# A new opening for a Perceiver layer kernel: the order of the first loads, of the first block's splitting and of the query rows

## What is computed

```python
qh = (q @ Wq.T + bq).reshape(B, Sq, N_HEAD, D_HEAD)      # q = layernorm(x), 128 x 256
kh = (k @ Wk.T + bk).reshape(B, Sk, N_HEAD, D_HEAD)      # k = v = context, 12544 x 256
vh = (v @ Wv.T + bv).reshape(B, Sk, N_HEAD, D_HEAD)
scores = jnp.einsum('bqhd,bkhd->bhqk', qh, kh) / np.sqrt(D_HEAD)
scores = jnp.where(attention_mask[:, None, :, :], NEG_FILL, scores)
probs = jax.nn.softmax(scores, axis=-1)
out = jnp.einsum('bhqk,bkhd->bqhd', probs, vh)
```

## Time and profile before

| | |
|---|---|
| median of 3 runs | 487.57 us (486.26 to 489.14) |
| profiled execution | 487.97 us, of which the span of its trace is 486.0 us |
| busy | PE 95%, DVE 58%, ACT 79%, POOL 21% |
| first phase | to about 240 us; DVE and PE near full |
| second phase | about 241 to 437 us; PE and ACT, DVE nearly idle |

### The profile page before, as it was taken

One profiled execution on the slowest core, in us unless ns is written; L12 is line 12 of the kernel. 1 busy time (PEld: TensorE's weight loads), 2 busy tenths in 40 slices (PEclk: granted clock), 3 DMA queues, 4 the chain that ended last, 5 costly groups with the idle time before them and its releaser, 6 DMA issues.

```text
span 486.0 us, 16042 instructions
## 1 busy us (share of the span) xinstructions
PE 462.6 (95%) x6479; PEld 367.2 (76%) x6485; DVE 282.0 (58%) x411; ACT 383.2 (79%) x425; POOL 102.1 (21%) x102
## 2 busy tenths in 40 slices
PE   6999999999999999997899999999999999999896
PEld 3876776777767677774388999999999999995463
DVE  5679999999999999999829900000000000004566
ACT  5387888888888888877288999999999999993423
POOL 4597323333233332324100000000000000000000
PEclk9899999999999999999799999999999999999999
DMA  8885578565786667985968777767887777500000
GB/s 266 305 299 232 213 306 316 227 247 220 293 324 228 242 229 280 331 334 215 372 255 327 280 251 272 283 269 284 320 325 279 273 265 261 229 3 2 1 1 13
DMA packets 34761, 117.50 MB, mean 242 GB/s; under 512 B 4400, under 2 KB 10416, under 8 KB 34736
## 3 DMA queue, kind: packets, MB, share of 16 engines
q1 hardware_dynamic: 30560, 110.58, 60.0%
q0 software_dynamic: 4032, 6.42, 4.4%
q10 hardware_dynamic: 144, 0.13, 0.1%
HBM read 74.44 MB, written 39.47 MB: 234 GB/s over the span
## 4 chain that ended last, share of the span: by engine, by line
PE 73%; DVE 8%; ACT 7%; issue 5%; POOL 4%; DMA 1%; ACTq 0%; SPq 0%; DVEq 0%; POOLq 0%
PE ps_a L1021 21%; PE ps_k L1034 19%; PE ps_a L877 11%; PE ps_k L868 11%; PE ps_a L911 6%; ACT early L474 4%; POOL k_stack L376 2%; DVE early L679 1%; DVE block_max L674 1%; ACT k_stack L437 1%; DMA early<-in_ctx 1%; POOL q_stack L404 1%; DVE early L710 1%; PE ps_a L1191 1%; PE ps_a L950 1%
## 5 line engine op out<-in xcount | busy, mean ns | idle before, releaser
L674 DVE TENSOR_REDUCE block_max<-ps_a 128x2 f32<-128x896 f32 x112 | 121.2, 1083 | 0.3
L1021 PEld LDWEIGHTS ps_a<-q_stack,k_stack 64*128 64x128 f32 x1568 | 96.2, 187 | 14.2 <-issue 12.5
L1021 PE MATMUL ps_a<-q_stack,k_stack 64*128 64x128 f32 x1568 | 105.5, 279 | 0.8 <-DVE q_stack L720 0.4
L474 ACT CAST early<-ps_a 128x896 bf16<-128x896 f32 x104 | 94.0, 904 | 7.7 <-PE ps_a L911 7.7
L531 ACT ACTIVATE middle<-ps_a 128x1536 f32<-128x1536 f32 (+1 forms) x56 | 90.2, 1662 | 9.9 <-PE ps_a L1021 9.9
L531 ACT ACTIVATE early<-ps_a 128x1536 f32<-128x1536 f32 (+1 forms) x56 | 90.2, 1663 | 5.5 <-PE ps_a L1021 5.5
L742 DVE COPY early<-ps_k 128x256 f32<-128x256 f32 x2 | 0.8, 419 | 158.9 <-PE ps_k L1034 158.9
L877 PE MATMUL ps_a<-w_hi,k_stack 128*128 128x256 f32 x392 | 68.6, 298 | 0.0
L679 DVE TENSOR_TENSOR early<-early 128x896 bf16<-128x896 bf16 x104 | 64.6, 621 | 0.0
L868 PE MATMUL ps_k<-k_stack,w_hi 128*128 128x448 f32 x224 | 61.0, 394 | 3.0 <-DVE w_lo L629 1.6
L877 PEld LDWEIGHTS ps_a<-w_hi,k_stack 128*128 128x128 f32 x392 | 53.3, 190 | 11.7 <-issue 11.6
(11 more groups left out here) (199 smaller groups left out, 468.5 us busy)
## 6 DMA issues: line engine op xcount, KB each, us to landing
k_stack<-k_hi_scratch SPq DMA_DIRECT2D x56, 448.0 KB, 6.0
v_scratch<-early SPq DMA_DIRECT2D x14, 952.0 KB, 5.7
v_in<-v_scratch SPq DMA_DIRECT2D x14, 952.0 KB, 7.9
k_hi_scratch<-k_hi SPq DMA_DIRECT2D x28, 448.0 KB, 2.9
k_lo_scratch<-k_lo SPq DMA_DIRECT2D x28, 448.0 KB, 3.4
k_stack<-k_lo_scratch SPq DMA_DIRECT2D x28, 448.0 KB, 6.2
early<-in_ctx SPq DMA_DIRECT2D x7, 896.0 KB, 7.6
ctx_b<-in_ctx SPq DMA_DIRECT2D x7, 896.0 KB, 7.6
```

What stands on the lines that cost most here:

```text
L474: nc.scalar.copy(staged[:, u % 2], pair_scores(u, 0)).then_inc(max_copied, 1)
L674: nc.vector.tensor_reduce(block_max[:, 2 * u:2 * u + 2, par], pair_scores(u, 1), AX.X, ALU.max).then_inc(max_taken, 1)
L1021: last = nc.tensor.matmul(ps_a[:, base + bank, at * Q:(at + 1) * Q], k_stack[half, b_par, a, t * P:(t + 1) * P], q_stack[half, a, ab, :], ...
```

## The change

- The loads: `wk` ahead of context block 0, block 0 in two halves of 448 rows (`first_in`), `bk` ahead of `bqn`, the mask in two halves, four row loads less (the bias rows `bqr`), no wait for the mask ahead of block 1, no wait for `low_context` behind the loads.
- The norm takes its root from ACT (`layernorm_by_root`), which loads the table of the square root, later that of the exponential with a dummy exponential behind it.
- Block 0 is split in four pieces of 448 columns, high parts on ACT, low parts all on DVE (`low_piece`), which also does its weights; POOL has no share of it. The first key projection waits for each piece as it comes.
- The query bias and scale move from DVE to ACT (`x3`). The queries are spread by 8 matmuls with an identity that ACT has spread by 4 (`eye_4`), in place of 16 with spread weights. ACT copies the result to `qr`.
- ACT makes the high part of block 1 in four pieces: two behind its second copy of values, then `qr`, then two.
- DVE looks for mask bits in two halves. PE reads the flag one slot later, after slot 8. `causal_b` is made later. POOL's two fills of `k_stack[:, 0]` move behind its split of block 2. `WARM_FIRST` is 9, `WARM_OPEN` 2.

The diff, cut to what the prediction speaks of:

```diff
-            sp.dma_start(ctx_t, ctx_d[0]).then_inc(ctx_in[0], 16)
             sp.dma_start(w_kv[:, 0:DC * D], wk_d.rearrange("p c n -> p (c n)")).then_inc(wk_in, 16)
+            for n in range(2):
+                half = slice(n * HK, (n + 1) * HK)
+                sp.dma_start(ctx_t.rearrange("p (c k) -> p c k", c=DC)[:, :, half], ctx_d[0][:, :, half]).then_inc(first_in[n], 16)
             sp.dma_start(w_kv[:, DC * D:], wv_d.rearrange("p c n -> p (c n)")).then_inc(wv_in, 16)
             sp.dma_start(wqn[:], wqn_d).then_inc(wqn_in, 16)
...
-            for slot in range(STRIDE):
-                sp.dma_start(bqr[slot::STRIDE, :], bqr_d[0:2 * HD, :]).then_inc(rows_in, 16)
-                if slot:
-                    sp.dma_start(row_mask[slot::STRIDE, 0:2], pairmask_d[0:2 * HD, :]).then_inc(rows_in, 16)
+            for slot in range(1, STRIDE):
+                sp.dma_start(row_mask[slot::STRIDE, 0:2], pairmask_d[0:2 * HD, :]).then_inc(rows_in, 16)
             sp.dma_start(row_mask[SLOTS::STRIDE, 2:4], pairmask_d[0:2 * HD, :]).then_inc(rows_in, 16)
-            sp.wait_ge(mask_all_in, 16)
             sp.dma_start(ctx_bufs[1], ctx_d[1]).then_inc(ctx_in[1], 16)
...
+            act.wait_ge(consts_set, 6)
+            nc.scalar.activation(stats[:, 20:21], magic[:, 0:1], ACT.Sqrt)
+            act.wait_ge(eye_in, 16)
+            nc.scalar.copy(eye_4.rearrange("p (n s) -> p n s", s=STRIDE),
+                           eye[:, :].unsqueeze(2).to_broadcast([P, P, STRIDE])).then_inc(eye_spread, 1)
+            root(1)
+            nc.scalar.activation(stats[:, 21:22], magic[:, 1:2], ACT.Exp)
+            high_weights(0, wk_in)
+            for n in range(PIECES):
+                act.wait_ge(first_in[n // 2], 16)
+                nc.scalar.copy(first_piece(ctx_hi[:, 0], n), first_piece(ctx_bufs[0].rearrange("p (c k) -> p c k", c=DC), n)
+                               ).then_inc(ctx_hi_ready, 1)
+            high_weights(1, wv_in)
...
+                        if first and work[1] == 1:
+                            high_piece(1, 1, 0)
+                            high_piece(1, 1, 1)
+                            act.wait_ge(q_projected, 2)
+                            nc.scalar.copy(qr.rearrange("p a q -> p (a q)"),
+                                           ps_a[:, 4:6, :].rearrange("p a n -> p (a n)")).then_inc(q_copied, 1)
+                            high_piece(1, 1, 2)
+                            high_piece(1, 1, 3)
...
             keep_clock(ps_v, WARM_OPEN)
+            pe.wait_ge(w_high, 1)
+            project(0, 0, 0)
             pe.wait_ge(transposed_copied, 1)
             pe.wait_ge(wqn_in, 16)
...
-            pe.wait_ge(wq_spread, 3)
+            pe.wait_ge(x3_ready, DC)
+            pe.wait_ge(eye_spread, 1)
             for a in range(PR):
-                for c in range(DC):
-                    last = nc.tensor.matmul(ps_a[:, 4 + a // 4, (a % 4) * Q:(a % 4 + 1) * Q], wq_rows(c, a, a + 1), xt[:, c, :],
-                                            start=(c == 0), stop=(c == DC - 1))
+                last = nc.tensor.matmul(ps_a[:, 4 + a // 4, (a % 4) * Q:(a % 4 + 1) * Q],
+                                        eye_4[:, (a % 4) * P:(a % 4 + 1) * P],
+                                        x3[:, (a // 4) * Q:(a // 4 + 1) * Q], start=True, stop=True)
```

202 lines of the change are left out of this document (100 added, 102 removed).

## The result

The changed kernel takes 482.89 us (median of 6 runs, 482.76 to 485.42) where the kernel before takes 488.11 on the same chip (6 runs, 486.26 to 489.14): a ratio of 0.9908 [0.9885, 0.9931], a gain of 4.5 us, taken over all runs of both; the two medians lie 5.2 us apart. Forecast were 3.3 us and 484.3. The execution that the profile shows took 485.42 us, the longest of the six, and its mean granted TensorE clock is 0.982, where the other five have 0.989 to 0.993. It isn't the execution that I had worked out. So I read it first for where it leaves the sum.

What follows compares the result with a forecast made beforehand. The block loop runs at DVE's pace, PE close behind; the opening, limited by ACT awaiting block 1's load, decides its start. Gain 3.6 less 0.3 for collisions gives 3.3 us, 487.57 to 484.3; 8-in-10 range 482.2 to 486.6.

Steps and rivals of the forecast that it cites:

- The mark: TensorE's first key matmul of block 1, the end of the opening; forecast to move from 29.69 to 26.1, gaining 3.6 us.
- The load of block 1 at 17.4: Opening: `ctx_b`, issued at 12.45, lands 5.0 us later and limits ACT; bounds 16.4 and 20.1.
- 8.2 us of ACT to 25.6: ACT's gapless work from block 1's landing to the last score copy, which PE's fourth score unit awaits.
- Slot 8 at 17.5: PE in the opening: slot 8 runs from 17.5 to 19.0, after the queries' identity matmuls and flag.
- first keys at 7.0: PE's first key matmul in the opening starts at 7.0 instead of 11.69 us.
- The fills at no cost, collisions 0.3: Block loop: POOL's moved fills cost DVE nothing; two delayed POOL pieces colliding with DVE cost 0.3 us, bounds 0 and 1.5.
- one stretch at 1.2 GHz in the sum, 1.2 us: PE between first keys and slot 8: low clock adds 1.2 us, bounds 0 and 2.4.
- 1.4 us of cover: Opening: by PE alone the mark would be 24.7, against 26.1 by ACT, so the clock stretch is covered.
- DVE is no limit there: From first keys to the mark: DVE's work ends at 17.2, just ahead of PE's flag matmul.
- rival 1: Block 1's load comes late, at 20.1; mark at 28.8, about 487.0 us, part of the way 486; chance 0.16.
- Rival 4: Slower: POOL's fills hold up DVE operations with two SBUF inputs in the third block, up to 6.2 us, 490.2; chance 0.04.
- rival 2: Block 1's load comes early, 16.4, and the clock is kept; mark 24.7 to 25.1, about 482.8 us; chance 0.10.

Runs made afterwards that it cites:

- e_fills: Changed kernel with POOL's two fills back at the start, ahead of its mask loads, instead of behind block 2's split; 483.14 us, ratio 0.9924.
- e_flag: Changed kernel with DVE setting the mask flag ahead of its three small row operations; 483.52 us, ratio 0.9924.
- e_all: Changed kernel with flag first, block 1's load ahead of causal mask and rows, fills at the start, 12 and 7 warm-up matmuls; 482.87 us, ratio 0.9911.
- e_cold: Changed kernel with 2 warm-up matmuls at the start and none behind the transposes, instead of 9 and 2; 484.63 us, ratio 0.9960.
- e_newton: Changed kernel with the first layer norm back on Newton steps on DVE and only the exponential's table loaded; 483.19 us, ratio 0.9921.
- e_warm: Changed kernel with seven warm-up matmuls behind the transposes instead of two; 482.79 us, ratio 0.9917.
- a_again: The changed kernel measured again with no edit; 484.19 us over 12 runs, ratio 0.9938 to the kernel before.
- e_flagctxb: Changed kernel with the flag ahead of DVE's row operations and block 1's load ahead of causal mask and rows; 482.80 us, ratio 0.9892.
- e_ctxb: Changed kernel with block 1's load issued ahead of the causal mask and the four row loads; 485.22 us, ratio 0.9948.
- e_late: Changed kernel with block 1's load issued behind the values' bias row and the self attention's weights; 486.42 us, ratio 0.9982.
- e_best: Changed kernel with flag first, block 1's load early, fills at the start, Newton norm, 9 and 4 warm-up matmuls; 485.59 us, ratio 0.9953.
- e_order: Changed kernel with the first loads in the old order, block 0 whole and ahead of the key weights; 486.90 us, ratio 0.9982.

## Why the prediction was right, and what it lacked

**All profiled executions in one table.** The mark against the time, in us; "rest" is the time less the mark, "ACT" the first cast of `ctx_b`, "u0" the first score unit.

| kernel | slot 8 | ACT | u0 | mark | mark - ACT | time | rest |
|---|---|---|---|---|---|---|---|
| e_fills | 17.09 | 16.65 | 18.52 | 24.81 | 8.16 | 481.73 | 456.9 |
| e_flag | 17.43 | 17.03 | 18.88 | 25.20 | 8.17 | 482.22 | 457.0 |
| e_all | 17.60 | 17.12 | 19.07 | 25.29 | 8.17 | 483.00 | 457.7 |
| e_cold | 17.90 | 17.30 | 19.41 | 25.47 | 8.17 | 484.14 | 458.7 |
| e_newton | 17.36 | 17.37 | 18.84 | 25.54 | 8.17 | 483.15 | 457.6 |
| e_warm | 17.48 | 17.59 | 18.95 | 25.76 | 8.17 | 482.79 | 457.0 |
| a_again | 17.58 | 17.87 | 19.03 | 26.03 | 8.16 | 483.52 | 457.5 |
| e_flagctxb | 19.43 | 18.06 | 21.20 | 27.06 | 9.00 | 484.01 | 456.9 |
| e_ctxb | 16.88 | 15.95 | 20.20 | 27.51 | 11.56 | 485.93 | 458.4 |
| e_late | 17.23 | 18.82 | 18.71 | 28.14 | 9.32 | 485.44 | 457.3 |
| e_best | 20.73 | 19.20 | 22.40 | 28.24 | 9.04 | 486.05 | 457.8 |
| after | 19.38 | 18.04 | 22.80 | 28.64 | 10.60 | 485.42 | 456.8 |
| before | 22.49 | - | 23.84 | 29.69 | - | 487.97 | 458.3 |
| e_order | 19.66 | 18.30 | 23.13 | 30.44 | 12.14 | 487.71 | 457.3 |

Three things can be read off. The time is the mark and 456.8 to 458.7 us, in every kernel: the marks differ by 5.6 us, the rests by 1.9, so the opening is most of what differs, but not all. Of the rest, the way from the mark to the end of the first phase took 209.7 to 210.4 us, and from there to the table load of the next norm 201.2 (e_fills) to 203.2 us (e_ctxb). That part runs the same program in all of them; why it varies by 2 us isn't known, and a single execution proves no difference of time below that. In the seven executions of the upper part the mark stands 8.16 or 8.17 us behind the cast, however the cast moves (over 1.22 us): the load of block 1 and ACT's work behind it set it, as forecast. In the lower part it stands 9 to 12 us behind: the flag, TensorE's late work or a clock that fell comes on top (e_late is the load's case still, with the clock on top).

**By the steps of the prediction.**

- The load of block 1 at 17.4, 8.2 us of ACT to 25.6, mark 26.1: measured 17.87, and 7.75 us to the fourth unit at 25.62, mark 26.03. The path is right, but the close hit on the mark is in part luck: the load was 0.47 us later and ACT's work 0.45 us shorter than in the sum. In the kernels that leave the load's place alone it was issued between 11.68 and 12.95 and took 5.0 to 5.6 us, so the forecast's 12.45 lies in the middle and its 5.0 at the short end.
- Slot 8 at 17.5, first keys at 7.0: 17.58 and 7.33. The first half of block 0 came at 6.62 instead of 6.2. The switch of tables, for which the Trainium skill (ScalarE: Activation LUTs, What ACT_TABLE_LOAD costs) has a drain of about 1.38 us besides the load, cost 1.29 with the load (4.12 to 5.41): the trace disagrees with the page, and e_newton shows that the switch is hidden anyway.
- The fills at no cost, collisions 0.3: 0.15 us. Against it, the old collisions of L701 and the first L695 changed: in the first profile from 0.86 and 1.38 to 0.19 and 0.62, so that the end of the first phase gained 1.62 us (240.05 to 238.43) behind a mark that had gained 1.05; in a_again they took 0.97 and 1.08, and the end gained 3.82 behind 3.66. I had no term for that; it lies between 0.2 and 0.6 us of gain. And the second phase, which I had held fixed, isn't: see above.
- The step that failed, in the late executions: "one stretch at 1.2 GHz in the sum, 1.2 us", bounded by 0 and 2.4, with "1.4 us of cover", and "DVE is no limit there". The stretch was nearly 7 us in the first profile, 5.5 in e_cold (by durations), and none in a_again. In e_cold it was covered. With loads about a microsecond late it puts slot 8 about 1.9 us late, past the cover; and then the two row operations, which I had not priced at all, fall beside POOL's split and hold the flag 1.4 us. The flag's way from DVE to TensorE's branch had no term either; in a_again slot 8 just hides it (flag set at 17.87, next matmul at 19.03). This is what the rivals lacked: rival 1 had a late mark by the load alone, and the profiled 28.64 came with the load in time.
- Rival 4 (fills that hold DVE) is wrong where the fills stand now, but a fill can hold a DVE operation, if not the kind that I named (two inputs): e_best shows it at the opening, on one with a single tensor as input.

Here the Trainium skill bears on the reading (SBUF — State Buffer, Who interferes with whom). By its rule a DVE instruction with two inputs in SBUF contends with a POOL instruction that reads SBUF; L680 and L682 are such, the trace agrees (0.83 and 0.89 instead of 0.15 us), and the rule names no size: two columns were held here as 896 were in the earlier trace rows. The same section has it that a `tensor_scalar` can run in a mode that takes both port pairs, and then blocks with POOL. By that, whichever of xn and a fill comes first holds the other, and the trace agrees (3.19 instead of 0.42 us). I had used the first half of the section for the fills' new place, and neither for the row operations nor, when I put the fills back, for the norm.

**The size of the gain.** 4.5 us [3.4, 5.6] in the first measurement, 3.0 [1.7, 4.3] in a_again, against 3.3 forecast. Both are mixtures: the share of late executions counts. In a_again 4 of 12 had the low mean clock of the first profile, and their mean, 487.02, is hardly below the 487.50 of the kernel before; in the first measurement it was one of six. By the rests of the table, an execution at the first median, 482.89, has its mark between 24.2 and 26.1, so from rival 2's case (load early) to the forecast's; none of those five was profiled. That the first measurement came out 1.4 us under the forecast is therefore not explained.

**What stays open.** Where the clock was low in an execution without a profile isn't known, only its mean, and the mean can miss a stretch, as in e_cold, where the profiled execution has 0.989 and another with 0.989 took 487.10 us. That 487.02 at 0.982 is the case of the first profile, which took 485.42, is inferred, not shown. Why the clock is kept in one execution and lost in the next isn't settled: in the profiles it was lost at the opening where PE had idled 1.32, 1.53 and 2.11 us just ahead of the first keys (after, e_flagctxb, e_order) or 3.58 ahead of the transposes (e_best), and kept where that was 0 to 0.89 us. That is no rule: PE also idled 1.94 us ahead of 22.80 in `after` and kept 1.00 behind it, and in e_cold 0.90 us stood ahead of slow matmuls at a column of 1.00. More warm-up work left one execution of seven at 487. Whether e_flagctxb is faster than `after` is open too: they ran on different chips, and [0.9862, 0.9921] overlaps [0.9885, 0.9931]. Against a_again, again on another chip, it looks better by 0.5%, and those intervals only just touch ([0.9862, 0.9921] and [0.9911, 0.9966]). The other parts of the change (low parts of block 0 all on DVE, the queries spread by the identity, the bias on ACT, block 1 in pieces) were not taken back one by one, so what each is worth isn't known.

## What to carry to other kernels

An opening is worth what its first block of steady work moves by, to within the scatter of what follows; fix such a mark and read the terms up to it. Order the loads by what the first consumer needs, and price each in two cases, in time and about two microseconds late: the cover that one case has may be gone in the other. Look for operations of a few columns that stand ahead of a flag or a branch: their size says nothing of their time when they fall beside another engine's work that holds them. And an edit that takes away one limit (e_ctxb) has to be made together with that of the next in line (the flag), or it may cost.
